# A loop over four batches written out: register counters and back edges against constants

## The reference

```python
q, k = apply_rope(q), apply_rope(k)
logits = jnp.einsum('bhid,bhjd->bhij', q, k) * SCALE
logits = jnp.einsum('bhij,gh->bgij', logits, Wpre)
attn = jnp.einsum('bhij,gh->bgij', softmax(logits), Wpost)
out = jnp.einsum('bhij,bhjd->bhid', attn, v) @ Wout.T + bout
x = layernorm(x + out)
# feed-forward: dispatch and combine are softmaxes of routing logits
slot_in = einsum('bnd,bnes->besd', layernorm(x) * gamma + beta, dispatch)
slot_out = gelu(slot_in @ w1 + b1) @ w2 + b2
x = layernorm(x + einsum('besd,bnes->bnd', slot_out, combine))
```

## Time and profile before

| | us |
|---|---|
| median of 3 runs | 8314.1 |
| the three runs | 8303.17, 8314.1, 8323.11 |
| the profiled execution | 8313.78 |
| its span, first to last instruction | 8311.6 |
| PE busy | 7998.6 |
| DVE busy | 7562.7 |
| ACT busy | 6886.2 |
| GpSimd busy | 6144.5 |

### The profile page before, as it was taken

How to read it: one execution, slowest core, us unless ns; L and a number is a source line. 1 busy time by engine, 2 the same in 40 slices (tenths; PEclk the granted TensorE clock), 3 DMA queues, 4 the chain that set the end, 5 groups by cost and what they waited for, 6 DMA issues and landing times.

```text
span 8311.6 us, 450171 instructions
## 1 busy us (share of the span) xinstructions
PE 7998.6 (96%) x182764; PEld 4651.1 (56%) x182764; DVE 7562.7 (91%) x13142; ACT 6886.2 (83%) x11772; POOL 6144.5 (74%) x12130
## 2 busy tenths in 40 slices
PE   7999999998899999999889999999989999999997
PEld 4555555555555555555545555555555555555554
DVE  7999999997899999999789999999978999999996
ACT  5888888886688898888568888888956988888884
POOL 6777778774677777777477777777747778777873
PEclk9999999998999999999899999999989999999998
DMA  1011111113101111111210111111121011111112
GB/s 53 24 28 26 27 26 28 26 27 91 34 25 26 28 26 26 28 27 26 90 35 25 26 28 26 27 27 27 26 89 36 25 26 28 26 28 26 27 26 92
DMA packets 265760, 284.09 MB, mean 34 GB/s; under 512 B 41088, under 2 KB 252672, under 8 KB 261376
## 3 DMA queue, kind: packets, MB, share of 16 engines
q1 hardware_dynamic: 263680, 255.07, 11.3%
HBM read 78.75 MB, written 39.85 MB: 14 GB/s over the span
## 4 chain that ended last, share of the span: by engine, by line
PE 81%; DVE 8%; issue 7%; POOL 2%; ACT 1%; DVEq 1%; POOLq 0%; DMA 0%; SPq 0%; ACTq 0%
PE psS L1262 53%; PE psP L1281 16%; PE psO L1296 6%; DVE big L900 3%; DVE pl L928 2%; PE psM L1307 2%; DVE spare L889 1%; PE psS L1392 1%; PE psS L1421 1%; PE psM L1322 1%; ACT big L707 1%; PE psS L1223 0%; PE psS L1210 0%; POOL at L488 0%; PE psM L1315 0%
## 5 line engine op out<-in xcount | busy, mean ns | idle before, releaser
L1262 PE MATMUL psS<-KH,AX 64*128 64x512 f16 x32768 | 3929.1, 377 | 52.1 <-DMA AX<-AX 50.1
L707 ACT ACTIVATE big<-psP 128x512 f16<-128x512 f32 x4096 | 2224.6, 596 | 832.0 <-PE psP L1281 829.0
L900 DVE SCALAR_TENSOR_TENSOR big<-psP,big 128x512 f16<-128x512 f32 x4096 | 2615.0, 680 | 182.5 <-ACT big L707 181.8
L688 ACT ACTIVATE pr<-psS,nb 128x1024 f32<-128x1024 f32 x2048 | 2293.5, 1120 | 99.0 <-DVE nb L889 87.3
L1262 PEld LDWEIGHTS psS<-KH,AX 64*128 64x128 f16 x32768 | 1450.2, 94 | 1516.1 <-DMA AX<-AX 51.7
L724 ACT ACTIVATE ph<-pr 128x1024 f16<-128x1024 f32 x2048 | 2169.5, 1059 | 32.4
L928 DVE TENSOR_TENSOR pl<-pr,ph 128x1024 f16<-128x1024 f32 (+1 forms) x2048 | 2121.0, 1036 | 0.0
L1262 PE MATMUL psS<-KL,AX 64*128 64x512 f16 x16384 | 2106.4, 376 | 0.0
L1281 PE MATMUL psP<-rh,ph 64*128 64x64 f16 x32768 | 1671.2, 191 | 87.4 <-DVE big L900 63.0
L1281 PEld LDWEIGHTS psP<-rh,ph 64*128 64x128 f16 x32768 | 1469.9, 95 | 498.8 <-DVE big L900 324.2
L1281 PE MATMUL psP<-rh,pl 64*128 64x64 f16 x32768 | 1668.2, 190 | 4.3 <-issue 3.9
(11 more groups left out here) (139 smaller groups left out, 6494.4 us busy)
## 6 DMA issues: line engine op xcount, KB each, us to landing
AX<-AX SPq DMA_DIRECT2D x2048, 64.0 KB, 2.0
ph<-in_xT SPq DMA_DIRECT2D x16, 512.0 KB, 8.8
xr<-in_x SPq DMA_DIRECT2D x64, 128.0 KB, 2.3
Q<-in_w SPq DMA_DIRECT2D x8, 1024.0 KB, 7.1
out<-V SPq DMA_DIRECT2D x16, 512.0 KB, 3.9
d_x<-x SPq DMA_DIRECT2D x60, 128.0 KB, 2.1
d_xn<-xn SPq DMA_DIRECT2D x60, 128.0 KB, 2.4
d_lg<-lg SPq DMA_DIRECT2D x60, 128.0 KB, 2.0
```

Source lines behind the costliest of these rows:

```text
L688: a.activation(pr[:, p, h * N2:(h + 1) * N2], psS[:, 2 * h:2 * h + 2, :].rearrange("p c n -> p (c n)"), ACT.Exp, bias=nb[:, p, h:h + 1], s ...
L707: a.activation(PT[:, hf * JH:(hf + 1) * JH, :, 0, i0:i0 + HQ], psP[:, ih, :].rearrange("p (j g i) -> p j g i", j=JH, g=H), ACT.Copy, scale ...
L900: v.scalar_tensor_tensor(out=PT[:, js, :, 1, i0:i0 + HQ], in0=psP[:, ih, :].rearrange("p (j g i) -> p j g i", j=JH, g=H), scalar=MDROP, in ...
L1262: mm = pe.matmul(psS[:, 2 * hp + half, :], AX[rows, k8, kq, s_, :], K_[rows, kq, hp, :], start=n == 0, stop=n == len(steps) - 1, tile_posi ...
```

## The change

The loop over the four batches is written out on GpSimd, ACT, DVE and PE as well: the Python loop emits the body four times with `b` = 0, 1, 2, 3. There is no counter in a register, no branch at the end of a pass, and no arithmetic in front of a wait; each wait carries a constant. The bodies, their order and the SP's program stay as they are.

```diff
@@ gpsimd
             barrier(g, 1)
-            with g.Fori(0, B) as b:
+            for b in range(B):
@@ scalar
             barrier(a, 1)
-            with a.Fori(0, B) as b:
+            for b in range(B):
@@ vector
             barrier(v, 1)
-            with v.Fori(0, B) as b:
+            for b in range(B):
                 v.memset(colmax[:, :], LOW).then_inc(s_dv, 1)
@@ tensor
             barrier(pe, 1)
-            with pe.Fori(0, B) as b:
+            for b in range(B):
                 pe.wait_ge(s_w, b * NW_DMA + NW_DMA)
```

## The result

The written-out kernel has a median of 8332.97 us (8324.3 to 8341.02) against 8316.19 us (8303.17 to 8323.57) before, with 14 executions of each: a ratio of 1.0021, 95% interval 1.0013 to 1.0029. It is 17 us slower. The forecast was 8301.5 us with a range of 8284 to 8316, so the time lies outside it, on the other side of "before".

What follows compares the result with a forecast made beforehand. The prediction took one long PE stream (busy 96%) as the bound, with PE idling at batch boundaries. Its sum was 8313.8 - 11.1 (boundaries) - 1.2 (register operations) = 8301.5 us, range 8284 to 8316.

Steps and rivals of the forecast that it cites:

- PE's back edge, 13.1 us in the open: At three batch boundaries PE, freed of its branch, starts up to 4.1, 5.3 and 3.7 us earlier, 13.1 in all.
- 11.1 us of it reach the end: At the boundaries, DVE and V's copies limit the gain: KH starts 3.05, 5.3 and 2.75 us earlier, 11.1 in sum.
- from KH on, these 3.05 us stay: At the first boundary, everything after KH hangs on it in one chain, so its 3.05 us gain is kept.
- The other back edges: cost now 0, gain 0: Branches of ACT, DVE and GpSimd fall in waits, under L1184's 5.25 us or before work arrives: gain 0.
- Register operations, 1.2 us, and middle parts unchanged: Operations before waits: 0.3 us a batch in the tails, 1.2 in all; 0 in middle parts, bounds 0 to 13 us.
- The code itself, 0: Four copies of PE's code are the same instruction stream without a jump: 0, or a few us either way.
- (c): GpSimd operations move under a DVE operation in each of 64 rows, as at L928: 34 us lost, 8335; chance 0.08.
- (a): The boundary gain is absorbed, or the branch only ends a wait that stays: 8313 to 8314 us; chance 0.15.
- (b): More than boundaries: a third of PE's L900 waits goes, 8281 us; milder, a warm clock, 8295; chance 0.17 together.

Runs made afterwards that it cites:

- pool_waits: Changed kernel, with GpSimd's first rope of a batch also waiting until DVE has ended the last normalization (L1184): 8308.19 us, ratio 0.9994.
- rest_only: Kernel before, with the loops of GpSimd, ACT and DVE written out and PE's loop kept: 8300.19 us, ratio 0.9979.
- loop_held: Kernel before, loops kept, one semaphore instruction added on PE between the wait for DVE's low half and the weight load: 8363.18 us, ratio 1.0051.
- pe_order: Changed kernel, with PE's last-met waits put first in the program, in the turn and the scores: 8306.79 us, ratio 0.9989.
- pe_only_order: Kernel before, with only PE's loop written out and PE's late waits put first in turn and scores: 8304.53 us, ratio 0.9981.
- both_fixes: Changed kernel, with GpSimd's first rope waiting for DVE's last normalization and PE's late waits put first in turn and scores: 8279.62 us, ratio 0.9952.

## Why the prediction was wrong, step by step

- **PE's back edge, 13.1 us in the open.** Right. The gap from W to PE's first matmul went from 4.26, 5.46 and 3.80 us to 0.05, 0.06 and 0.05, and the first eight matmuls take 3.70 us instead of 5.31. The row bears out the rule of the Trainium skill that was followed ("Runtime: NRT & Kernel Launch", Instruction fetch mechanics), that a taken branch to a target outside the loaded pages stalls until the page is there: the gap went with the jump.
- **11.1 us of it reach the end.** Right as far as KH, once there is no collision: with PE's loop alone written out (pe_only) KH came 11.4 us earlier in sum. But only 7.4 of these reached the first scores, so the step "from KH on, these 3.05 us stay" does not hold for PE's share alone. In pool_waits the boundaries are 10.8 us shorter than before, with the other engines' loops gone too (rest_only alone: 3.8); that this is so near 11.1 is in part luck. KH was forecast at W + 15.8, 15.7 and 15.7 and came there at 15.77, 16.13 and 15.79, again partly by chance: V's copy began at W + 13.63 instead of the forecast W + 14.57, and the collision with L857 then took 0.99 us.
- **The other back edges: cost now 0, gain 0.** This is the first step that failed. The times were looked at as costs only. ACT's jump and table load, hidden in ACT's own idle time, also held GpSimd back until DVE had finished L1184. The prediction took L1184 as 5.25 us in every version; it measured 11.17. The step did not ask what an earlier producer lets run sooner, and beside what.
- **Register operations, 1.2 us, and middle parts unchanged.** The second failed step, in two directions. As to cost they were mis-sized: rest_only gained 17.0 us (10 to 25 by its interval) where the sum had 1.2 in all. This is above the 14.2 of the upper bound (13 in the middle parts) and the 1.2 together, though not clear of noise, and how much of it is register operations and how much the back edges, set at 0, is open. Nor are the 3.8 us of its boundaries sure: loop_held, with every loop kept, has boundaries of 185.3 us, 2.5 less than before. And they had a side effect that was not in the sum at all: they decided which of PE's waits stood on the weight load. That is worth 26 us (pe_order against after). With all four loops written out and the wait in its place, the middle parts are 7735.1 us, 18.9 less than before; with the wait on the sequencer they are 13.9 more. PE's loop alone, with the wait in its place, gives 0.5 of the 18.9 (pe_only_order, 7753.5), and the other three 4.4; the traces do not say where the rest comes from.
- **The code itself, 0.** Not separated. No run shows that four copies as such cost anything; pe_order and both_fixes have them and are faster than before.
- **Rivals.** (c) had the right mechanism for one of the two causes, a GpSimd operation moving under a DVE operation, in the wrong place: it sought L928 in each of 64 rows, whose mean did not change (1036 ns before, 1035 after), and it is L1184 at three boundaries. That its time (8335) is near is luck; it has no term for the held wait. (a) is refuted by pool_waits. (b) is true for the part that rest_only shows in its one trace, 8 us less waiting for L900.

In sum, relative to before: about -11 for the boundaries without collision, about +23 for the collision (25 by pool_waits against after, 23 by the interaction of the halves), and the rest, by difference some +5, from the gain of the loops' other costs and the loss of the held wait (26 us), which nearly cancel.

What stays open. Why the held sequencer costs as much as it does is argued, not shown. One reading fits the traces: it can't run ahead of the weight loads, so PE's next block of code is asked for later. Counted from the records of turns and outputs, PE's stalls of over 80 ns at every 256th instruction sum to 43.1 us (87 of them) before, 47.6 (107) after and 32.9 (74) in pe_order. That is 14.7 of the 32.8 us between the last two; the first eight matmuls of turns (202.5 us after, 193.5 in pe_order, from start to start) and of scores (1512.0 and 1500.0) are slower too, while the step from a turn to the next scores is 10.6 us shorter in sum. How rest_only's gain divides among the three engines and among register operations, back edges and waits was not tried, nor was a rope order that keeps clear of L857 as well.

## What to carry to other kernels

When an edit lets one engine start earlier, follow its consumers on to the engine that shares a resource with the one on the critical path; an idle stretch that costs nothing may be what keeps two of them apart. When an edit turns computed waits into constants, or moves or merges waits, look at which wait ends up on the instruction itself and which on a semaphore instruction before it. Try the one that is met last first in the program, where it stayed on the weight load here; it was worth 26 us in the turns and nothing in the scores. If PE's idle time in front of a weight load changes from another engine to "issue" while the totals of PE's waits stay the same, the wait has moved to the sequencer.

## What the runs showed of the hardware that was not expected

- A 128 x 256 float32 tensor_scalar on DVE of 0.41 us took 1.35 to 1.43 us under a GpSimd tensor_tensor of 128 x 512 (1.26 to 1.42 us), one stretched DVE operation for each GpSimd operation; a 128 x 512 tensor_tensor of 0.69 us took 1.81.
- A wait for the same semaphore at the same point of PE's program costs 26 us of 8333 more over some 2044 uses, 13 ns each, when a semaphore instruction of 51 ns carries it instead of the weight load. With register loops, where that instruction was added for it, the two together cost 45 us.
- PE's three taken branches lasted 3.4 to 4.9 us each. ACT's, of 45 ns, was followed by 2.8 us without an instruction (2096.78 to 2099.57), and GpSimd's, of 50 ns, by 6.0 us (2040.39 to 2046.42).
